# Two-layer decoder on one core: both transposes ahead of both products in the expert loop, and a third S^T bank in the narrow attention

## What is computed

```python
def _L0_xattn_ref(q, k, v):
    qh = q.reshape(B, S, KV, G, D).transpose(0, 2, 3, 1, 4)
    kh = k.reshape(B, S, KV, D).transpose(0, 2, 1, 3)
    vh = v.reshape(B, S, KV, D).transpose(0, 2, 1, 3)
    scores = jnp.einsum('bkgsd,bktd->bkgst', qh, kh) / scale
    weights = jax.nn.softmax(scores, axis=-1)
    out = jnp.einsum('bkgst,bktd->bkgsd', weights, vh)
...
def _L1_ffn_ref(hidden_states, ...):
    ...
    xs = x_exp[sort_idx]
    g = jax.lax.ragged_dot(xs, w_gate, group_sizes)
    u = jax.lax.ragged_dot(xs, w_up, group_sizes)
    d = jax.lax.ragged_dot(jax.nn.silu(g) * u, w_down, group_sizes)
    ...
    expert_out = jnp.sum(out * weights[..., None], axis=1)
    shared = jax.nn.silu(x @ sw_gate) * (x @ sw_up) @ sw_down
    return (expert_out + shared).reshape(B, S, H)

x = _layernorm(x + _L0_attn_ref(x, ...))
x = _layernorm(x + _L0_xattn_ref(x, ctx_512, ctx_512))
x = _layernorm(x + _L0_ffn_ref(x, ...))
x = _layernorm(x + _L1_attn_ref(x, ...))
x = _layernorm(x + _L1_xattn_ref(x, ctx_512, ...))
x = _layernorm(x + _L1_ffn_ref(x, ...))
```

## Time and profile before

| | |
|---|---|
| median of the runs | 943.18 us (939.62 to 945.26) |
| the profiled execution | 945.49 us, span 943.7 us |
| granted TensorE clock, mean | 0.912 |
| busy: PE / DVE / ACT / POOL | 770.0 / 493.4 / 303.7 / 208.2 us |
| first joined attentions | about 42 to 265 us |
| first feed-forward block | 266 to 355 us |
| second joined attentions | 355 to 620 us |
| routing and shared units | 620 to 695 us |
| expert loop | 696 to 905 us |
| combine | 905 to 944 us |

### The profile page before, as it was taken

How to read it: one execution, slowest core, us unless ns; L and a number is a source line. 1 busy time by engine, 2 the same in 40 slices (tenths; PEclk the granted TensorE clock), 3 DMA queues, 4 the chain that set the end, 5 groups by cost and what they waited for, 6 DMA issues and landing times. The chain is left out here.

```text
span 943.7 us, 18324 instructions
## 1 busy us (share of the span) xinstructions
PE 770.0 (82%) x6877; PEld 470.4 (50%) x6877; DVE 493.4 (52%) x1319; ACT 303.7 (32%) x703; POOL 208.2 (22%) x267
## 2 busy tenths in 40 slices
PE   4599987777829968999999999787759999999910
PEld 3467765555515534565565666555524444444400
DVE  6655655666227873454553555329943333333337
ACT  0012233444320000233333333323225555555500
POOL 3201111111000010000000000032235666666410
PEclk9999999999559985899999999959979999999965
DMA  9492000000020000000000000059012222222263
GB/s 302 124 280 68 2 3 1 2 2 2 2 89 1 0 0 1 2 1 2 1 2 1 1 2 2 1 147 264 3 39 74 85 89 86 85 90 85 73 214 115
DMA packets 48123, 55.28 MB, mean 59 GB/s; under 512 B 7366, under 2 KB 43174, under 8 KB 47334
## 3 DMA queue, kind: packets, MB, share of 16 engines
q1 hardware_dynamic: 38246, 34.11, 12.3%
q0 software_dynamic: 6656, 16.85, 5.4%
q10 hardware_dynamic: 3136, 3.15, 1.0%
HBM read 41.45 MB, written 12.65 MB: 57 GB/s over the span
## 5 line engine op out<-in xcount | busy, mean ns | idle before, releaser
L609 DVE TENSOR_REDUCE nmf<-bank 128x4 f32<-128x512 f32 x192 | 123.7, 686 | 137.9 <-PE bank L295 137.7
L495 ACT ACTIVATE pt<-bank 128x512 f32<-128x512 f32 x192 | 104.2, 595 | 251.5 <-PE bank L315 251.5
L295 PE MATMUL bank<-kk,qT 32*128 32x256 f32 x768 | 114.5, 417 | 15.2 <-ACT pt L495 8.3
L726 POOL TENSOR_TENSOR rstd<-vare,half 128x1 f32<-128x1 f32 x32 | 17.6, 550 | 436.7 <-DVE vare L670 436.7
L295 PEld LDWEIGHTS bank<-kk,qT 32*128 32x128 f32 x768 | 70.2, 193 | 53.5 <-issue 36.8
L1467 PE MATMUL bank<-g_wgu,g_xgT 128*64 128x352 f32 x256 | 91.4, 481 | 0.0
L1467 PE MATMUL bank<-wgu,g_xgT 128*64 x256 | 91.4, 480 | 0.0
L315 PE MATMUL bank<-nm,sel 32*128 32x128 f32 x768 | 85.7, 341 | 0.0
L307 PE MATMUL bank<-qT,kk 32*128 32x512 f32 x256 | 77.0, 679 | 1.7 <-ACT pt L495 1.4
L1432 POOL DMA_INDIRECT out_rows<-g_og,g_out_row x64 | 63.1, 986 | 59.3 <-DVE g_og L1536 56.4
L1487 PE MATMUL bank<-wd,g_hT 128*64 x256 | 68.9, 392 | 0.1
(11 more groups left out here) (250 smaller groups left out, 1392.3 us busy)
## 6 DMA issues: line engine op xcount, KB each, us to landing
wgu<-in_L_ffn_w_gate SPq DMA_DIRECT2D x4, 1408.0 KB
wgu<-in_L_ffn_w_up SPq DMA_DIRECT2D x4, 1408.0 KB
wd<-in_L_ffn_w_down SPq DMA_DIRECT2D x32, 176.0 KB
g_y<-out_rows SPq DMA_DIRECT2D x4, 768.0 KB, 12.4
g_y<-out_rows ACTq DMA_DIRECT2D x4, 768.0 KB, 15.8
sparse_table<-f_m_re SPq DMA_DIRECT2D x2, 1024.0 KB, 6.4
f_m_re<-sparse_table SPq DMA_DIRECT2D x2, 1024.0 KB, 5.8
f_idx_row<-in_L_ffn_mask_idx SPq DMA_DIRECT2D x1, 1024.0 KB
```

The source lines that it names most:

```text
L295: return pe.matmul(bank, q, k, start=first, stop=r == 1, skip_group_check=True)
L495: act.activation(T.pt[2 * (t % 2) + u][:, :], STB[u][:, :], ACT.Exp, scale=own[v].scale).then_inc(exp_done, 1)
L609: dve.tensor_reduce(T.nmf[v % 2][:, 2 * (c % 2) + u, at:at + 4], SB[u][:, :].rearrange("p (h k) -> p h k", h=4), AX.X, ALU.max, negate=Tru ...
```

## The change

**In the expert loop** step c now issues on TensorE the x transposes of slot c + 2, the h transposes of slot c, gate/up of slot c + 1 and the down product of slot c. ACT does the index load for c + 2, the x copy of c + 2, the h copy of c, the weight copy of c + 2 and silu of c + 1. DVE does the multiply of c + 1, the output copy of c and the weight copy of c + 2; POOL the gather of c + 5 and the scatter of c.

**In the narrow attention** of the first joined stage the S^T halves of v >= 9 go in turn through three banks, the third being M, and from v = 10 on a half waits for the exponential of the half three before it (in place of two). At the first pair of v = 9 TensorE also waits for the residual of v = 7, the last user of M.

```diff
-        SB, STB = T.SB, T.STB
+        SB = T.SB
+
+        def st_bank(v, c, u):
+
+            if own[v] is not CROSS0:
+                return T.STB[u]
+            return [*T.STB, M][(2 * (before[v] + c) + u) % 3] if v > B else T.STB[u]
+
+        def emptied(v, c, u):
+
+            unit = 2 * (before[v] + c) + u
+            return unit - 2 if own[v] is CROSS0 and v > B + 1 else unit - 1
...
+                    if own[v] is CROSS0 and v == B + 1 and i == 0:
+                        pe.wait_ge(res_done, B)
                     for u in range(2):
                         if p > 0:
-                            pe.wait_ge(exp_done, 2 * (p - 1) + u + 1)
+                            pe.wait_ge(exp_done, emptied(v, i, u))
...
@@ -1426,7 +1439,7 @@
                         pool.wait_ge(xt_done, n - 3)
                     pool.indirect_dma_start(G.xg[n % 4][:], None, G.x_rows[:, :],
                                             bass.IndirectOffsetOnAxis(ap=G.x_row[:, n:n + 1], axis=0)).then_inc(gathered[n % 4], 16)
-                n = c - 1
+                n = c
                 if has(n):
                     pool.wait_ge(out_ready, n + 1)
                     pool.indirect_dma_start(G.out_rows[:, :], bass.IndirectOffsetOnAxis(ap=G.out_row[:, n:n + 1], axis=0),
@@ -1455,6 +1468,14 @@
                     for j in range(KT):
                         last = pe.transpose(trx[n % 2][:, j * 128:(j + 1) * 128], G.xg[n % 4][:, j * 128:(j + 1) * 128], T.ident[:])
                     last.then_inc(xt_done, 1)
+                n = c
+                if has(n):
+                    pe.wait_ge(h_ready, n + 1)
+                    if n >= 2:
+                        pe.wait_ge(ht_ready, n - 1)
+                    for j in range(2):
+                        last = pe.transpose(trh[n % 2][0:MH, j * 128:(j + 1) * 128], G.h[n % 2][:, j * MH:(j + 1) * MH], T.ident[:])
+                    last.then_inc(tr_done, 1)
                 n = c + 1
                 if has(n):
                     pe.wait_ge(xt_copied, n + 1)
@@ -1469,14 +1490,6 @@
                     last.then_inc(gu_done, 1)
                 n = c
                 if has(n):
-                    pe.wait_ge(h_ready, n + 1)
-                    if n >= 2:
-                        pe.wait_ge(ht_ready, n - 1)
-                    for j in range(2):
-                        last = pe.transpose(trh[n % 2][0:MH, j * 128:(j + 1) * 128], G.h[n % 2][:, j * MH:(j + 1) * MH], T.ident[:])
-                    last.then_inc(tr_done, 1)
-                n = c - 1
-                if has(n):
                     pe.wait_ge(ht_ready, n + 1)
                     if n >= 2:
                         pe.wait_ge(out_ready, n - 1)
@@ -1500,22 +1513,22 @@
             def step(c):
                 n = c + 2
                 if has(n):
+                    unit = act.value_load(G.unit[0:1, SHARE * n + 1:SHARE * n + 2], min_val=0, max_val=UNITS - 1)
                     act.wait_ge(xt_done, n + 1)
                     act.activation(G.xgT[n % 2][:], trx[n % 2][:, 0:D], ACT.Copy).then_inc(xt_copied, 1)
+                n = c
+                if has(n):
+                    act.wait_ge(tr_done, n + 1)
+                    act.activation(G.hT[n % 2][0:MH, :], trh[n % 2][0:MH, 0:256], ACT.Copy).then_inc(ht_ready, 1)
+                n = c + 2
+                if has(n):
+                    if n >= 2:
+                        act.wait_ge(gu_done, n - 1)
+                    act.activation(G.wgu[n % 2][:], T.wgu[:, bass.ds(unit, 1), :, :].rearrange("p a k n -> p (a k) n"), ACT.Copy).then_inc(wgu_ready, 1)
                 n = c + 1
                 if has(n):
                     act.wait_ge(gu_done, n + 1)
                     act.activation(G.sil[n % 2][:], gu[n % 2][:, 0:MI], ACT.Silu).then_inc(sil_ready, 1)
-                n = c
-                if has(n):
-                    act.wait_ge(tr_done, n + 1)
-                    act.activation(G.hT[n % 2][0:MH, :], trh[n % 2][0:MH, 0:256], ACT.Copy).then_inc(ht_ready, 1)
-                n = c + 3
-                if has(n):
-                    if n >= 2:
-                        act.wait_ge(gu_done, n - 1)
-                    unit = act.value_load(G.unit[0:1, SHARE * n + 1:SHARE * n + 2], min_val=0, max_val=UNITS - 1)
-                    act.activation(G.wgu[n % 2][:], T.wgu[:, bass.ds(unit, 1), :, :].rearrange("p a k n -> p (a k) n"), ACT.Copy).then_inc(wgu_ready, 1)
 
             act.wait_ge(T.low_loaded, T.low_count)
             act.wait_ge(T.high_loaded, T.high_count)
@@ -1528,13 +1541,13 @@
                 if has(n):
                     dve.wait_ge(sil_ready, n + 1)
                     dve.tensor_tensor(G.h[n % 2][:], gu[n % 2][:, MI:2 * MI], G.sil[n % 2][:], ALU.mult).then_inc(h_ready, 1)
-                n = c - 1
+                n = c
                 if has(n):
                     dve.wait_ge(down_done, n + 1)
                     if n >= 4:
                         dve.wait_ge(scattered[n % 4], landed(n, 1))
                     dve.tensor_copy(G.og[n % 4][:], down_bank[n % 2][:, 0:D]).then_inc(out_ready, 1)
-                n = c + 1
+                n = c + 2
                 if has(n):
                     if n >= 2:
                         dve.wait_ge(down_done, n - 1)
```

10 lines of the change are left out of this document (5 added, 5 removed).

## The result

| | before | changed |
|---|---|---|
| median us (20 runs each) | 942.27 | 950.65 |
| lowest to highest | 938.12 to 947.65 | 941.48 to 956.58 |
| profiled execution | 945.49, span 943.7 | 951.51, span 949.6 |

The ratio of changed to before is 1.0063, 95% interval 1.0040 to 1.0086: 0.6% slower, where 923.4 us and a faster kernel were predicted.

The account below looks back on a forecast made before the run. TensorE's order was taken to bound the expert loop, and ACT the narrow attention. Loop 16.7 plus bank 3.1 made 19.8 us: 945.49 to 925.7 profiled, the median 2.3 lower, so 923.4 us; range 917.5 to 932.5.

Parts of the forecast that it names:

- The expert step: TensorE's step in the expert loop: 2.78 us in place of 3.06, 17.1 us less over 61 steps.
- the ends: Start and end of the expert loop: 1.5 us lost before slot 2's gate/up, 1.1 gained after slot 63's.
- The bank: Third S^T bank in the narrow attention: two fills per sample gain 0.22 us each; 3.1 us in all, bounds 0 to 6.6.
- The wait for the residual at v = 9: Narrow attention: this wait is on work of v = 7, claimed long done by then.
- the pair of the earlier trace: Narrow attention, pair at 197.2: ACT's exponentials end at 198.72, holding TensorE, with DVE only 0.22 us behind as a limit.
- The other engines must follow at 2.78: Expert loop: ACT needs 1.85 us a step, POOL 2.56, and h comes with 0.3 us of slack, so they keep up.
- its 0.81 wait for the output copy is slack: Expert loop, POOL: beyond gather and scatter, 2.56 us a step, its 0.81 us wait was taken as spare time.
- the DMAs are as many, a tenth denser: Expert loop: the number of DMAs stays the same and they come a tenth closer together; no cost was given.
- Rival (b): Expert loop: h late; handovers 0.15 longer each give 934, 0.3 later each step nears 3.06, 940; chances 0.06 and 0.04.
- the clock (d): Expert loop: waits for h drop TensorE's granted clock, making the kernel slower; 955 us at 16 such slots; chance 0.03.
- Rival (a): Expert loop: first down weights can't load behind a gate/up pass, exposing 0.14 per slot, 8.7 us; 932.1; chance 0.08.
- Rival (c): Narrow attention: the bank does nothing, as DVE's reduce or wake-up takes the same moment; 926.5; chance 0.05.

Follow-up runs that it names:

- both_sp: Changed kernel with each slot's gather and scatter issued by SyncE as plain transfers between fixed rows, GpSimd idle in the loop; 923.71 us, ratio 0.9800.
- scatter_sp: Changed kernel with the scatters alone issued by SyncE as plain transfers to fixed rows, gathers staying on GpSimd; 933.75 us, ratio 0.9881.
- no_gather: Changed kernel with the first four gathers alone, later slots working on those rows; 928.54 us, ratio 0.9857.
- bank_only_again: Kernel before with the third S^T bank alone, run again on another chip beside more runs; 952.15 us, ratio 0.9951.
- before_events: Kernel before with SyncE adding 1 to an unused semaphore sixteen times in each slot; 958.32 us, ratio 1.0040.
- bank_only: Kernel before with the third S^T bank alone, without the new expert order; 949.70 us, ratio 0.9946.
- light_waits: Kernel before with the third bank, and three already covered waits of TensorE's step taken out; 940.15 us, ratio 0.9943.
- deep: Changed kernel with h transposes and down pass taken one slot later, copies and scatters moved with them; 953.44 us, ratio 1.0123.
- before_extra: Kernel before with one more indirect gather behind every fourth slot's scatter, into a tile nobody reads; 974.11 us, ratio 1.0336.
- before_itself: Kernel before, unchanged, run for its own profile on this chip; 945.59 us, ratio 0.9994.
- paced: Changed kernel with the scatter moved one step back and made to wait for the gate/up pass of slot n+2; 946.53 us, no interval.

## Why the prediction was wrong

**The expert step** was priced right: 2.78 in every undisturbed slot, and 2.784 in the mean of both_sp, scatter_sp and no_gather. So were the ends. Slot 2's gate/up starts 9.33 behind the first x transposes, where 707.24 - 699.48 = 7.76 stood before: 1.6 lost, 1.5 predicted (the terms that the prediction writes out give 708.2, 0.9 lost; what brings it to 708.7 is not said there, so this hit is in part luck). Slot 63's gate/up to the last output copy is 905.76 - 901.44 = 4.32, predicted 4.2. The test of the step is the slots alone: 169.6 us from slot 2 to slot 63 in both_sp against 186.6 before, 17.0 less, predicted 17.1. That both_sp's whole gain, ratio 0.9800 or 18.8 us of 942.27, comes near the sum of 19.8 tests nothing: its interval reaches from 12.5 to 25.3, and its profile is 24.5 us shorter, some 4 of them behind slot 63's gate/up, where its rows are other rows.

**The bank** was given 3.1, and the changed kernel's narrow attention ends 2.5 earlier (255.01 against 257.47) and its expert stage starts 2.2 earlier. The size is near, its terms are not. Three fills of the changed kernel:

```profile
166.19 0.48 PE L306 MATMUL bank<-kk,qT 32*128 32x256 f32 x2 [1.28 <-DVE res L674]
...
194.00 0.48 PE L306 MATMUL bank<-kk,qT 32*128 32x256 f32 x2 [0.49 <-DVE nmf L622]
...
200.79 0.49 PE L306 MATMUL bank<-kk,qT 32*128 32x256 f32 x2 [0.75 <-ACT pt L508]
```

The wait for the residual at v = 9, "long done then" in the prediction, is not: TensorE stands 1.28 us there, 0.53 more than the 0.75 before. One fill per sample moves to DVE's end and gains 0.26 (194.00 is 12.48 behind the same fill of the sample before, formerly 12.74), not two by 0.22. The other, which is the pair of the earlier trace rows, gains nothing: it starts 0.35 behind the maxima's increment in both kernels (200.44 to 200.79 here, 198.51 to 198.86 before), so what held it was not ACT's end, which the row names, but TensorE's own waits behind the maxima, 0.11 us apart. From the start of sample 9 to the attention's end no_gather, whose clock changes within some 1 us of where it does before, gains 2.65: 5 x 0.26, about 0.5 in the last score fill and 1.3 around sample 15, less the 0.53. That the sum came near is luck.

Alone the bank gains about 0.5%, 4.7 to 5.1 us, in two groups. What is beyond the 2.5 goes with the clock of the stretch from 120 to 268 us, which differs from execution to execution. The stretch in the kernel before, in the changed kernel's profile, and in bank_only_again's:

```profile
120.00:268.00 148.00, 114.37 (x1520) 80.65 (x1518) 77.74 (x185) 54.53 (x115) 21.95 (x43) 0.89 0.01 2
```

```profile
120.00:268.00 148.00, 113.39 (x1525) 80.62 (x1524) 78.29 (x186) 54.91 (x116) 21.93 (x43) 0.89 0.03 8
```

```profile
120.00:268.00 148.00, 104.75 (x1513) 75.61 (x1516) 79.55 (x185) 58.52 (x117) 21.94 (x43) 0.93 0.05 16
```

In the last of them, with a granted clock of 0.93, the attention's last exponentials start at 248.43, nine us ahead of the kernel before's. Four profiles of kernels with the bank end there near 249, all at 0.93 or 0.94; those without it end at 255 to 262, also the one of before_events at 0.94. The runs on record say the same: the whole execution's granted clock is 0.919 or more in 19 of 56 executions of the changed kernel, bank_only, bank_only_again and light_waits, and in 7 of 101 of the kernel before. That the bank makes the higher level more frequent is likely from this; why is not shown.

**The step that failed** is the paragraph "The other engines must follow at 2.78". Its durations hold. But every handover from TensorE was taken as some 0.03 us behind its cause, as the earlier trace rows have it at 3.07 us a slot, and nothing asked whether the news itself could be late. GpSimd was judged by its busy time: 2.56 of 2.78 us, "its 0.81 wait for the output copy is slack". That wait spaced the transfers. The sentence "the DMAs are as many, a tenth denser" is where the cost lay: where the kernel before takes 942 to 945 us, two indirect transfers in its 3.07 us leave TensorE's increments in time, and two in 2.78 do not. The increments came about 1.06 us late in every second slot against a slack of 0.3, so the mean step is 3.19 in place of 2.78, and the loop gives back 25.2 us, more than the whole gain. That the transfers do it is shown by taking them away and by adding some; by what path is not.

**Rival (b)**, h late, is the nearest: h is late, but not by three handovers of 0.15. It was priced only up to a step near 3.06, at which nothing is lost; nothing in its own working stops there, and the measured 1.06 in one handover goes with a step of 3.66. As a slower case only the clock (d) had been thought of, and the changed kernel's clock is 1.00. **Rival (a)** is refuted: the down product starts 0.30 behind a gate/up pass, its weights loaded beside it, in the same rows of the array:

```profile
806.54 0.14 PEld L1500 LDWEIGHTS bank<-wd,g_hT 128*64 128x64 f32 x1 [0.15 <-issue]
```

By the Trainium skill, TensorE: Matmul & The Clock Gate, The mechanism, a load overlaps a running matmul only in another row group, though the same section also has one into the background weight buffer pulled ahead; this trace disagrees with the first, here as at 893.62 before. **Rival (c)** is refuted by bank_only. The Trainium skill, TensorEngine Tiling, Key Properties, says that a change of tiling mode drains TensorE, without a price; the trace agrees in kind: with two mode changes fewer the plain step is 0.28 shorter, 0.14 each.

## To carry to other kernels

Where one engine's step is made shorter, count for every other engine not only its busy time but how many indirect transfers and increments now fall into each microsecond: here two indirect transfers and eleven increments of engines in 3.07 us went through where the kernel before takes 942 to 945 us, and in 2.78 did not. Judge by slack as well: where it takes 953 to 955, kernels with its loop had late increments in half of their slots and yet only 8 or 9 long ones, since their order could take them up. The sign of it is an engine that idles on TensorE's increment although the timeline shows the pass long over; here one step more of distance for h (deep) did not help then, because the next handover was late too; fewer indirect transfers did. When a saving eats the slack of a second resource that was never the bound, the outcome can be a loss, not a smaller gain, as here.

## What the hardware showed that was not expected

TensorE's increments can come late while TensorE itself goes on, by up to 1.8 us in the changed kernel and up to 4.8 in before_extra, and 0.04 to 0.09 us apart once they are let go (bank_only). In the changed kernel none of ACT's and DVE's that its trace kept were. Rows, bytes and GpSimd's busy time are not what counts; indirect instructions are (at a plain step of 2.78, 0 or 1 a slot: none late; 1.75: 3.00 a slot; 2: 3.10 to 3.39 over all groups; 2 and a plain one: 3.43; and 2.25 in 3.07: 3.45), and plain increments likely count somewhat. In the kernels with late increments the trace has also lost most records of the semaphores' increments: between 710 and 880 us 627 of the transfers' increments stand in the changed kernel's trace against 1744 before and 1890 in both_sp. Lost records alone do not slow a kernel down (before_itself has 533 and no long slot). What the shared path is, and whether the recording of events has a part in it, no run here tells. The other open points are the two levels of one kernel on one chip (945 and 955 us), and whether two indirect transfers that really stand apart would do better, since paced did not part them.
